# An attention and mixture-of-experts kernel: maxima turned by VectorE, parts moved from one product to another, new orders

## The reference

```
x = x + xattn(layernorm(x), ctx)        # x: 4 batches x 256 tokens x 256, ctx: 4 x 256 x 256
x = x + ffn(layernorm(x))

xattn: Q = x @ Wq.T + bq; K, V likewise from ctx; 16 heads of 16
       softmax(Q K.T / 4) V, then @ Wo.T + bo
ffn:   8 experts of 32, top 2 by softmax(x @ G)
       out = sum over experts of w_e * (silu(x @ gate_e) * (x @ up_e)) @ down_e
           + sum over experts of w_e * (x @ A_e) @ B_e      # low rank, 16 each
```

## Time and profile before

| | us |
|---|---|
| median of 3 runs | 115.64 (114.97 to 116.44) |
| profiled execution: its own time | 115.25 |
| profiled execution: its span | 113.5 |
| TensorE (matmul) busy | 104.7 (92%) |
| VectorE busy | 89.8 (79%) |
| ScalarE busy | 70.8 (62%) |
| GpSimd busy | 61.5 (54%) |

### The profile page before, as it was taken

How to read it: one execution, slowest core, us unless ns; L and a number is a source line. 1 busy time by engine, 2 the same in 40 slices (tenths; PEclk the granted TensorE clock), 3 DMA queues, 4 the chain that set the end, 5 groups by cost and what they waited for, 6 DMA issues and landing times.

```text
span 113.5 us, 2548 instructions
## 1 busy us (share of the span) xinstructions
PE 104.7 (92%) x868; PEld 79.6 (70%) x868; DVE 89.8 (79%) x185; ACT 70.8 (62%) x127; POOL 61.5 (54%) x91
## 2 busy tenths in 40 slices
PE   4976999997999999999999999979998899999990
PEld 4656868775776766758676696858565889888680
DVE  5454199998989899799999996968599765589941
ACT  0414562389899869878888899897963504335110
POOL 2268910499859803990588746482729981442000
PEclk9999999999999999999999999999999999999999
DMA  2994788762498003910000400000000000110034
...
DMA packets 9405, 11.91 MB, mean 105 GB/s; under 512 B 1008, under 2 KB 6448, under 8 KB 9392
## 3 DMA queue, kind: packets, MB, share of 16 engines
...
...
## 4 chain that ended last, share of the span: by engine, by line
PE 66%; DVE 10%; DMA 7%; POOL 5%; issue 5%; ACT 3%; SPq 1%; POOLq 0%; DVEq 0%
PE unit L766 18%; PE unit L872 12%; PE unit L840 9%; PE unit L773 8%; PE unit L859 7%; DMA wa<-wattn 4%; DMA qstack<-q_lo 3%; POOL attnT L491 3%; PE unit L913 2%; PE unit L911 2%; PE unit L912 2%; DVE rowmax L695 2%; POOL attnT_lo L492 2%; PE unit L846 1%; PE unit L799 1%
## 5 line engine op out<-in xcount | busy, mean ns | idle before, releaser
L695 DVE TENSOR_REDUCE rowmax<-unit 128x4 f32<-128x1024 f32 x32 | 37.5, 1212 | 1.7 <-PE unit L840 1.5
L604 ACT ACTIVATE probs<-unit 128x1024 f32<-128x1024 f32 x32 | 32.2, 1030 | 4.7 <-PE unit L859 4.4
L872 PE MATMUL unit<-probs,vaug 128*32 128x256 f32 x256 | 15.9, 383 | 0.0
L840 PE MATMUL unit<-kstack,qstack 63*128 63x256 f32 x128 | 14.1, 311 | 0.8 <-DVE rowmax L695 0.4
L840 PEld LDWEIGHTS unit<-kstack,qstack 63*128 63x128 f32 x128 | 9.6, 185 | 5.9 <-issue 3.0
L859 PE MATMUL unit<-qstack,kstack 64*128 64x256 f32 x128 | 13.3, 300 | 0.2
L491 POOL TENSOR_SCALAR attnT<-attnT,bias_sb 128x256 f32<-128x256 f32 x8 | 7.7, 957 | 8.6 <-ACT attnT_hi L541 8.2
L859 PEld LDWEIGHTS unit<-qstack,kstack 64*128 64x128 f32 x128 | 9.6, 185 | 3.6 <-issue 1.5
L627 ACT COPY hlT<-unit 128x384 f32<-128x384 f32 x8 | 3.7, 479 | 12.7 <-PE unit L906 12.7
L872 PEld LDWEIGHTS unit<-probs,vaug 128*32 128x32 f32 x256 | 7.3, 109 | 5.1
L459 POOL TENSOR_SCALAR vare<-mv 128x2 f32<-128x2 f32 x8 | 1.8, 223 | 13.2 <-DVE mv L645 12.9
...
## 6 DMA issues: line engine op xcount, KB each, us to landing
kstack<-k_hi SPq DMA_DIRECT2D x8, 256.0 KB, 2.7
qstack<-q_hi SPq DMA_DIRECT2D x6, 256.0 KB, 2.8
xs<-x SPq DMA_DIRECT2D x4, 256.0 KB, 3.4
kstack<-k_lo SPq DMA_DIRECT2D x4, 256.0 KB, 2.7
...
cT<-ctxT SPq DMA_DIRECT2D x3, 256.0 KB, 3.7
qstack<-q_lo SPq DMA_DIRECT2D x3, 256.0 KB, 2.9
...
```

The costliest lines, as they stand in the source:

```text
L604: act.activation(probs[:, n % NPAIR], unit[PAIR[name, n] // 2][:], ACT.Exp, scale=SCALE).then_inc(exp_done, 1)
L695: dve.tensor_reduce(rowmax[:, b % 2, :, i // 4, :, i % 4].rearrange("p t j -> p j t"), unit[PAIR[name, n] // 2][:], AX.X, ALU.max)\
L840: ins = pe.matmul(dst[:, j, t], qs[rows, PLACE[i], t * P:(t + 1) * P], ks[rows, PLACE[i]], start=True, stop=True)
L872: ins = pe.matmul(dst[QUAD * j:QUAD * (j + 1), i], vaug[:, of % 3, t, 4 * g + j], probs[:, n % NPAIR, j % 2, t], start=(t == 0), stop=(t = ...
```

## The change

- `mrow` leaves TensorE and ScalarE. `rowmax` becomes fp32r and is padded with zeros (by GpSimd in `ones`) to 32 columns for each half of the tokens; VectorE turns it by four transposes for each `mrow`, one for each block of 32 partitions, each 32x64, all written to partitions 0 to 31 of `mT`. There are 32 such transposes in all.
- `ahi`, `alo`, `wohi` and `wolo` go: `o` takes `attnT` and `wo` as float32, two products for each half of the tokens in place of six in parts. The bias of V goes through Wo once: a new stage `bias` of two products on TensorE (the bias broadcast as weights) and one addition by VectorE into `bo_sb`; `xo` waits for it.
- `down` of batches 0, 1 and 2 is in parts: 9 products in fp32r in place of 3 in float32. The rounded part of `hlT` is written by ScalarE as before, the rest by a new subtraction of VectorE (`hl`, from a 128x384 block in PSUM); the weights are split once (`outshi` by ScalarE, `outslo` by GpSimd). `down` of batch 3 stays in float32.
- `c:0` and `wk` are loaded whole. `x:0` is issued by ScalarE's queue; on SyncE's queue `c:0`, `wk`, `wq` and `wo` come first, and `wv` only after the first stacking of keys.
- All five orders are new. On TensorE, `k:2`, `k:3` and `v:1` are earlier, and `u:5`, `glu0:0` and `attn:3.0` to `3.2` stand before `max:3.7`.

The diff, cut: of the orders, what the text speaks of.

```diff
+
...
     "tensor": """
-        k:0@0 xT:0@1 qh:0@1 qh:1@0 k:1@2 v:0@1 max:0.0@4 max:0.1@6 xT:1@2 max:0.2@0 max:0.3@4 q:1@2 v:1@3
-        mrow:0.0@0 max:0.4@4 max:0.5@6 max:0.6@0 k:2@2 max:0.7@4 attn:0.0@6 xT:2@3 attn:0.1@0 max:1.0@6
-        attn:0.2@4 mrow:0.1@3 attn:0.3@0 max:1.1@6 max:1.2@4 q:2@3 max:1.3@0 max:1.4@6 attn:0.4@4 k:3@2
...
-        attn:3.0@6 u:5.0@0 u:5.1@0 attn:3.1@2 attn:3.2@4 attn:3.3@6 mrow:3.1@1 glu0:0@0 x2T:1@1 glu1:0@2
-        o:2@3 attn:3.4@0 attn:3.5@4 low:1@2 attn:3.6@6 attn:3.7@0 u:6.0@3 u:6.1@3 u:7.0@2 u:7.1@2 x2T:2@3
-        glu0:1@0 hl:0@1 glu1:1@2 hl:1@3 low:2@4 o:3@0 down:0@1 glu1:2@0 hl:2@2 down:1@3 x2T:3@2 down:2@4
-        glu0:2@5 hl:3@2 low:3@4 glu1:3@1 glu0:3@2 hl:4@0 down:3@4 hl:5@0 down:4@5 hl:6@0 down:5@2 hl:7@0
-        down:6@1 down:7@0
+        k:0@0 xT:0@1 bias:0@2 qh:0@1 qh:1@0 k:1@3 v:0@1 max:0.0@4 max:0.1@6 xT:1@0 v:1@2 max:0.2@0 max:0.3@4
+        max:0.4@6 q:1@3 k:2@2 max:0.5@0 max:0.6@4 k:3@6 xT:2@7 max:0.7@0 attn:0.0@2 max:1.0@4 q:2@7 max:1.1@0
+        attn:0.1@2 max:1.2@4 v:2@6 max:1.3@0 attn:0.2@2 max:1.4@4 u:0.0@7 attn:0.3@2 max:1.5@0 xT:3@6
+        max:1.6@4 attn:0.4@2 u:0.1@7 attn:0.5@0 max:1.7@2 attn:0.6@4 q:3@6 max:2.0@0 attn:0.7@4 max:2.1@2
+        u:1.0@7 max:2.2@0 attn:1.0@4 u:1.1@7 max:2.3@2 attn:1.1@4 attn:1.2@0 v:3@6 max:2.4@2 attn:1.3@0
+        max:2.5@4 o:0@7 attn:1.4@0 max:2.6@2 attn:1.5@4 u:2.0@6 attn:1.6@0 max:2.7@2 attn:1.7@4 u:2.1@6
+        attn:2.0@0 attn:2.1@2 max:3.0@4 u:3.0@7 u:3.1@7 max:3.1@0 attn:2.2@4 attn:2.3@2 u:4.0@6 x2T:0@0
+        max:3.2@4 attn:2.4@2 u:4.1@6 attn:2.5@0 max:3.3@4 attn:2.6@2 o:1@7 max:3.4@0 attn:2.7@2 max:3.5@4
+        u:5.0@6 u:5.1@6 max:3.6@0 attn:3.0@2 attn:3.1@4 glu0:0@7 low:0@2 attn:3.2@0 max:3.7@4 glu1:0@3
+        x2T:1@2 o:2@6 low:1@2 attn:3.3@4 attn:3.4@0 attn:3.5@6 glu0:1@2 attn:3.6@4 attn:3.7@0 u:6.0@3 u:6.1@3
+        u:7.0@4 u:7.1@4 hl:0@5 x2T:2@0 hl:1@1 glu1:1@2 o:3@0 low:2@3 glu0:2@2 glu1:2@0 hl:2@1 hl:3@3 x2T:3@4
+        down:0@5 down:1@2 low:3@4 glu0:3@1 down:2@0 hl:4@2 down:3@3 hl:5@4 glu1:3@1 down:4@2 hl:6@4 down:5@5
+        hl:7@1 down:6@3 down:7@2
...
     "vector": """
-        minus:0 ln1:0 norm1:0 ln1:1 k:0 qh:0 k:1 qh:1 max:0.0-3 ln1:2 q:1 max:0.4-7 max:1.0 ln1:3 max:1.1-7
-        u:0 max:2.0-3 u:1 max:2.4-7 u:2 max:3.0 o:0 max:3.1-2 ln2:0 max:3.3 u:3 max:3.4-5 u:4 max:3.6 o:1
-        ln2:1 max:3.7 u:5 route1:0 route2:0 glu0:0 glu1:0 o:2 ln2:2 route3:0 route1:1 u:6 u:7 route2:1 glu0:1
-        route3:1 glu1:1 o:3 ln2:3 route1:2 norm2:3 route2:2 down:2 route3:2 down:0 glu0:2 glu1:2 route1:3
-        route2:3 route3:3 glu0:3 weigh:6 glu1:3 weigh:7 down:4 down:3 down:5 down:6 down:1 down:7
+        minus:0 ln1:0 norm1:0 ln1:1 k:0 qh:0 bias:0 qh:1 k:1 max:0.0-1 ln1:2 max:0.2-3 mrow:0.0 max:0.4 q:1
+        max:0.5-7 max:1.0 ln1:3 max:1.1-2 mrow:0.1 max:1.3-5 mrow:1.0 max:1.6 u:0 max:1.7 max:2.0-1 mrow:1.1
+        max:2.2-3 u:1 max:2.4 mrow:2.0 max:2.5 o:0 max:2.6 ln2:0 max:2.7 u:2 max:3.0 mrow:2.1 max:3.1 u:3
+        max:3.2 u:4 max:3.3 mrow:3.0 max:3.4-5 o:1 ln2:1 max:3.6 u:5 max:3.7 route1:0 mrow:3.1 route2:0
+        glu0:0 o:2 glu1:0 ln2:2 route3:0 route1:1 route2:1 glu0:1 u:6 u:7 route3:1 hl:0 glu1:1 o:3 ln2:3
+        route1:2 hl:1 norm2:3 glu0:2 route2:2 route3:2 hl:2 down:1 down:0 glu1:2 hl:3 route1:3 route2:3
+        glu0:3 route3:3 hl:4 weigh:6 hl:5 glu1:3 weigh:7 down:3 down:5 down:2 down:4 down:6 down:7
...
     """,
     "sync": """
...
+        c:0 wk wq wo x:1 c:1 obias khi:0 wv klo:0 qloh:0 qhih:1 qloh:1 x:2 khi:1 klo:1 c:2 x:3 c:3 mstack:0.0
+        qhi:1 qlo:1 wf khi:2 klo:2 outs mstack:0.1 qhi:2 qlo:2 mstack:1.0 khi:3 qhi:3 qlo:3 mstack:1.1
+        mstack:2.0 klo:3 mstack:2.1 mstack:3.0 mstack:3.1 out:0 out:1 out:3 out:5 out:4 out:2 out:6 out:7
     """,
...
-        mT = sb("mT", [PAIRS, 2, S], F32R)
+        rowmax = sb("rowmax", [P, 2, 2, ST, QUAD], F32R)
+        mT = sb("mT", [QUAD, 2, ST, P], F32R)
...
-            if b == 0:
-                engine.dma_start(cT[:, 0, 0], ctxT[0, 0:P]).then_inc(c_in[0], 16)
-                return
...
-            if name == "wk":
-                engine.dma_start(wa[:, 0, at], wattn[0:P, at]).then_inc(wk_in, 16)
-                return
...
-            if name == "cb":
-                engine.dma_start(cT[:, 0, 1], ctxT[0, P:D]).then_inc(c_rest_in, 16)
-            if name == "wkb":
-                engine.dma_start(wa[:, 1, 0:D], wattn[P:D, 0:D]).then_inc(wk_rest_in, 16)
...
-                wait_freed(engine, "mrow", 2 * b + i)
+                engine.wait_ge(max_rows, 2 * b + i + 1)
                 engine.dma_start(qstack[b % NSTACK][ROWS:P:HALF].bitcast(F32).rearrange("j (p k) t -> j p k t", k=KT)[:, :, i],
-                                 mT[:, i].bitcast(F32)).then_inc(m_stacked[b % NSTACK][i], 16)
+                                 mT[0:PAIRS, i].bitcast(F32).rearrange("c t p -> c (t p)")).then_inc(m_stacked[b % NSTACK][i], 16)
...
+                if name == "outslo":
+                    pool.wait_ge(wd_hi_ready, 2)
+                    pool.tensor_tensor(wd_lo[:], wd[:], wd_hi[:].bitcast(F32), ALU.subtract).then_inc(wd_parts, 1)
+                    pool.tensor_tensor(lb_lo[:], lb[:], lb_hi[:].bitcast(F32), ALU.subtract).then_inc(wd_parts, 1)
+                    pool.wait_ge(wd_parts, 2)
...
-                if name == "wolo":
-                    pool.wait_ge(wo_hi_ready, 1)
-                    pool.tensor_tensor(wo_lo[:], wo[:], wo_hi[:].bitcast(F32), ALU.subtract).then_inc(wo_parts, 1)
-                    pool.wait_ge(wo_parts, 1)
-                if name == "alo":
-                    of, k = b // 2, b % 2
-                    pool.wait_ge(attn_hi_ready, b + 1)
-                    sums = attnT[:, of % 2, k]
-                    link(pool.tensor_scalar(sums, sums, bv_sb[:, k:k + 1], None, ALU.add))
-                    pool.tensor_tensor(attnT_lo[:, k], sums, attnT_hi[:, k].bitcast(F32), ALU.subtract)\
-                        .then_inc(attn_parts, 1)
-                    pool.wait_ge(attn_parts, b + 1)
...
+                    pool.memset(rowmax[:, :, :, :, PAIRS:QUAD].bitcast(F32), 0.0).then_inc(row_pads, 1)
+                    pool.wait_ge(row_pads, 1)
...
-                    pool.wait_ge(out_bias_in, 16)
+                    wait_freed(pool, "bias", 0)
...
-                if name == "wohi":
-                    act.wait_ge(wo_in, 16)
-                    act.copy(wo_hi[:], wo[:]).then_inc(wo_hi_ready, 1)
-                if name == "ahi":
-                    of, k = b // 2, b % 2
-                    act.wait_ge(bias_in, 16)
-                    act.wait_ge(attn_ready, b + 1)
-                    if of:
-                        wait_made(act, "o", of - 1)
-                    act.activation(attnT_hi[:, k], attnT[:, of % 2, k], ACT.Identity, bias=bv_sb[:, k:k + 1])\
-                        .then_inc(attn_hi_ready, 1)
...
+                if name == "outshi":
+                    act.wait_ge(wd_in, 32)
+                    act.copy(wd_hi[:], wd[:]).then_inc(wd_hi_ready, 1)
+                    act.copy(lb_hi[:], lb[:]).then_inc(wd_hi_ready, 1)
...
-                if name == "mrow":
-                    bank, turn = WORK[name, 2 * b + i]
-                    wait_made(act, name, 2 * b + i)
-                    if b:
-                        act.wait_ge(m_stacked[(b - 1) % NSTACK][i], 16 * ((b - 1) // NSTACK + 1))
-                    act.copy(mT[:, i], work[bank][0:PAIRS, 0]).then_inc(work_free[bank], 1)
...
-                    act.copy(hlT[:, b % 2].rearrange("p k s -> p (k s)"),
-                             work[bank][:].rearrange("p h s -> p (h s)")[:, 0:EF + P]).then_inc(work_free[bank], 1)
+                    in_parts = b // 2 in DOWN_PARTS
+                    act.copy((hlT_hi if in_parts else hlT)[:, b % 2].rearrange("p k s -> p (k s)"),
+                             work[bank][:].rearrange("p h s -> p (h s)")[:, 0:EF + P])\
+                        .then_inc(hl_hi_ready if in_parts else work_free[bank], 1)
...
+                if name == "bias":
+                    wait_made(dve, "bias", 0)
+                    dve.wait_ge(out_bias_in, 16)
+                    dve.tensor_tensor(bo_sb[:], work[bank][:, 0], bo_sb[:], ALU.add).then_inc(work_free[bank], 1)
...
-                    dve.tensor_reduce(rowmax[:, b % 2, :, i // 4, :, i % 4].rearrange("p t j -> p j t"), unit[PAIR[name, n] // 2][:],
+                    of_pair = rowmax[:, b % 2, i // 4, :, 0:PAIRS].rearrange("p t (j c) -> p j t c", c=4)[:, :, :, i % 4]
+                    dve.tensor_reduce(of_pair, unit[PAIR[name, n] // 2][:],
                                       AX.X, ALU.max)\
                         .then_inc(max_done, 1)
+                if name == "mrow":
+                    if b:
+                        dve.wait_ge(m_stacked[(b - 1) % NSTACK][i], 16 * ((b - 1) // NSTACK + 1))
+                    dve.wait_ge(max_done, PAIRS * b + 4 * i + 4)
+                    dve.wait_ge(row_pads, 1)
```

(76 more changed lines are left out.)

51 lines of the change are left out of this document (17 added, 34 removed).

## The result

The changed kernel took 118.67 us (median of 4, 118.37 to 119.92), the kernel before 115.31 beside it: a ratio of 1.033 (95% interval 1.028 to 1.039). It is slower by 3.4 us, outside the range of the prediction. The profiled execution took 118.91 for a span of 117.2.

What follows compares the result with a forecast made beforehand. TensorE sets the end, with VectorE only 2.7 us from full in the attention stretch. The last maximum comes 6.7 later, is won back afterwards, and the end moves from 110.87 to 110.3: -0.6, 115.0 us, range 112.0 to 117.6.

Steps and rivals of the forecast that it cites:

- Its start: Start of the attention stretch: `wv`, moved behind the first stacking, delays VectorE's first maximum to 15.95, +0.65 (0 to 1.5).
- I take 0.20: VectorE's 32x64 transposes for `mrow`: 0.20 us each, 0.8 for one `mrow` (0.6 to 1.0), 5.6 for seven.
- Rival 1: Slower: VectorE's transposes run one by one at 0.25 each, +1.6 on its path, giving 116.6; chance 0.28.
- the hold: VectorE's transposes: input starting in another group of 32 partitions waits until all earlier instructions finish, so each costs full length.
- From it to the last product of `u`: After the last maximum: from `attn:3.4` to the last product of `u` 6.1 us, as before, ending at 86.2.
- A second weighing: VectorE's doublings beside GpSimd's attention subtractions (0.84 for 0.42) go, leaving the sum some tenths lower.
- VectorE's 16.3 us after `o:3`: Tail: 16.4 before, plus 2.5 for five `hl` subtractions, idle cut from 3.2 to 0.6; `weigh:7` ends at 106.9.
- decides: Tail: VectorE's path, ending at 110.3, is later than TensorE's sum at 109.6 and so sets the end.
- Rival 3: Start: whole `wk`, two queues and moved `wv` cost 1.5 to 2 more than the 0.65, giving 116.8; chance 0.08.

## Why the prediction was wrong

Its steps, and what the profiled execution after shows (us from the span's start):

| step | predicted | measured | lost since the step before |
|---|---|---|---|
| first maximum | 15.95 | 17.14 | 1.2 |
| last maximum ends | 76.3 | 78.66 | 1.2 |
| `attn:3.4` | 80.1 | 81.81 | -0.7 |
| last product of `u` ends | 86.2 | 90.03 | 2.1 |
| `o:3` ends | 90.6 | 94.40 | 0 |
| `weigh:7` ends | 106.9 | 110.89 | 0.2 |
| last addition starts | 110.3 | 114.18 | -0.1 |

- "Its start ... VectorE start at 15.95: +0.65 (0 to 1.5)" failed. The loads were costed and not the pace. Loads came 0.9 earlier than assumed, and TensorE's first products ran at half pace: +1.84. With 16 warm-ups the first maximum is at 15.89, so at full pace the forecast place would have been right. Why the pace stays low in one execution and not in another is open.
- "I take 0.20: 0.8 for one `mrow`" was mis-sized: 0.97, or 7 x 0.17 = 1.2 in the stretch. Rival 1, with the hold, had this price right and was given 0.28. The kernel with all four on the same partitions shows the mechanism: it gives back 2.5 for 0.36 less on each `mrow`. That the 1.2 lost in the stretch are just this price is a match of size: VectorE was busy for 59.12, as summed (59.05), and the excess is in its idle time, 2.4 instead of 1.3, of which 1.0 are waits for scores. With 16 warm-ups the stretch is 60.7.
- "From it to the last product of `u` were ... 6.1" failed: from `attn:3.4` to there are 8.2. The row itself was faster than forecast, 1.8 from its issue at 79.98 to `attn:3.4` for 2.7. But `attn:3.5` then waited 1.41 us for VectorE to clear its bank of `o:2`, and that addition stood behind the 1.38 us instruction beside GpSimd. In the kernel without GpSimd's reads the wait is 0.32 (82.08). The other 0.7 is not accounted for. "A second weighing" expected collisions with GpSimd to go with its attention subtractions. They moved: the remaining subtractions for `x2T_lo` took 1.95 us of the tail.
- From there on the sum held within 0.4 us: VectorE's 16.3 us after `o:3` came out at 16.5, and the five subtractions of `hl` at 0.5 each are in it. That VectorE "decides" there is not shown: without them the tail was 0.5 us longer, not shorter.
- The last addition to the span's end took 3.0 instead of 2.6; with that the 4.3 us of span are complete.
- Rival 3's "later orders can't win it back, since VectorE is full" held: 1.25 us at the first maximum were 2.0 at the end. Its cause did not: the loads were early, and the start was late by its pace. Rival 1's price and a start as late as half of rival 3's came together. The prediction gave both at once 0.09, but worked out no time for it and ended its range below: 116.6 + 1.2 would have been 117.8, and the wait at `attn:3.5` was in no rival.
